# Second attention in blocks of one key block, values in four strips of 32 columns, and limits chosen head by head

## The chip, the core and the metric

The kernel runs on one core of a Trainium2 chip. The metric is the device time of one execution in microseconds (us). The engines are TensorE (PE in rows; PEld are its weight loads), VectorE (DVE), ScalarE (ACT), GpSimd (POOL) and SyncE, which only issues DMAs here. They run on their own and meet at semaphores.

## The reference, cut to what matters

The program is a model of two layers over 2 sequences of 1024 tokens with 1024 features: a token map, attention, a mixture of experts, and the same two again. The change is in the attention of the second layer, which keeps only the 128 highest scores of each row:

```python
draft = jnp.einsum('bhqd,bhkd->bhqk', qr, kr)
draft = draft + jnp.where(causal_future, neg, 0.0)
_, draft_indices = jax.lax.top_k(draft, 128)
mask = jnp.full((B, H, Sq, Sq), neg, dtype)
mask = mask.at[b_idx, h_idx, s_idx, draft_indices].set(0.0)
mask = jnp.where(causal_future[None, None, :, :], neg, mask)
scores = jnp.einsum('bhqd,bhkd->bhqk', qr, kr) / np.sqrt(HD) + mask
out = jnp.einsum('bhqk,bhkd->bhqd', jax.nn.softmax(scores, axis=-1), v)
```

There are 32 heads of 32 features in each sequence, four to a group of keys and values.

## The kernel before

`kept_attention` (from L825) works on pairs of heads, 32 pairs in all. For each head a row tile i (128 queries, i from 0 to 7) has i + 1 key blocks of 128 columns. The pairs pass through a pipeline of four stages, and one **slot** of the program does all four for four different pairs, so that 30 slots of 32 have every stage: *score* the pair s + 1, *search* the limits of pair s, *keep* (rank, choose and mark) pair s - 1, and *value* pair s - 2.

A slot is cut into five **passes**, 0 to 4. In each, ScalarE counts for 12 row tiles how many scores lie above a trial limit (`count`, L1076), VectorE then corrects the limits (`narrow`, L1253 to L1283, 11 short instructions in passes 1 to 3), and ScalarE's next count waits for that (`t_ready`). After pass 4 there is no correction: VectorE works out the first limits of the next pair instead (`start`, L1228 to L1249), from statistics of its scores (`gather`, L1226). ScalarE and VectorE thus take turns five times a slot, and whatever VectorE still has to do when a count ends makes the next count late.

Into the counts of passes 0, 1 and 2 ScalarE puts the evacuations of the value stage (`evac`, L1044): the exponential of a *chunk*, from one of two PSUM banks (`ps_t`) to SBUF (`probT`). There are 24 chunks in a slot, eight to a pass, of which five stand among the counts and three behind the last of them. A chunk before is up to four key blocks of one row tile of one head, and the chunks stand in pairs of the two heads. Their widths in blocks of 128 are 1, 1, 2, 2, 3, 3, 4, 4 in pass 0, 4, 4, 1, 1, 4, 4, 2, 2 in pass 1 and 4, 4, 3, 3, 4, 4, 4, 4 in pass 2.

TensorE fills a chunk (`turn`, L976): it transposes the score blocks, adds the negative maximum of each row (`row_of` times `topT`, L984) and adds the mask, transposed too (L989). A turn waits until the chunk two before it is evacuated. Behind each pair of turns stand the values of the pair before (`values`, L1001): [V | ones], 64 columns of weights for each head, times a 128-column block of `probT`, in float32; the two heads use the two halves of the array's columns. The profile has each float32 matmul as two rows. Among the turns of pass 2 TensorE also scores the first row tiles of the pair s + 1, two at a time ahead of the turns 16, 18 and 20, and the rest after its last values. The scores have two large banks (`ps_s`), and TensorE waits until VectorE has copied the tile two before (`fetch`, L1346, and `x_ready`).

VectorE's other work in a slot: it ranks (`rank_some`, L1297 on; L1291 and L1294 for each row tile) 8 of 14 tiles in pass 0 and 6 in pass 1, fetches scores 0 to 5, learns whether any row failed (`any_failing`) and marks 10 tiles (`mark`, L1338) in pass 2, marks 4, fetches 6 to 11 and copies the output in pass 3, and fetches 12 to 15 in pass 4. Fetches of passes 3 and 4 have statistics (`gather`) between them. GpSimd chooses the limits of all 14 tiles at once (`choose`, L1100), from the end of the ranking on, and later splits the row maxima in three parts (`split_top`, L1151). These are turned by TensorE and brought to SBUF by ScalarE at the end of pass 3 (`top_evac`, L1046), for the turns of the next slot.

A line number of GpSimd or VectorE names the instruction, and L1257 is the first of a correction, L1283 its last, L1244 the one that releases the first count of a slot.

## Time and profile before

| | us |
|---|---|
| median of 3 runs (lowest to highest) | 5007.57 (5001.28 to 5016.76) |
| the profiled execution | 5014.9 |
| its span | 5013.0 |
| PE busy in the span | 4052.5 (81%) |
| DVE busy | 3267.8 (65%) |
| ACT busy | 2800.5 (56%) |
| POOL busy | 311.6 (6%) |

The span begins with the first instruction of the profile and ends with the last. The page has a line for each engine with the busy tenths of 40 slices: in those of the second attention ACT and DVE stand at 7 and 8 tenths, PE at 6 and 7, and the clock granted to TensorE at 7 and 8 tenths. A timeline row has start, duration, engine, line, what is written and read, and how many instructions it merges; in brackets stands how long the engine was idle before, and who released it.

### The profile page before, as it was taken

The page shows a single profiled execution, that of the slowest core. Times are in us where ns is not written, and L with a number is a line of the kernel's source. Part 1 is how long each engine was busy: PE and PEld are TensorE (multiplying, and loading weights), DVE is VectorE, ACT ScalarE, POOL GpSimd, SP SyncE. Part 2 cuts the span into 40 slices and gives each one's busy share as a digit, 9 for nine tenths or more (in the row PEclk, how much of TensorE's full clock was granted, in tenths as well). Part 3 has the DMA queues.
Part 4 walks back from the last instruction along what each step waited for, and adds up shares of the span by engine and source line. Part 5 has one row for each costly group of instructions (what it writes and reads, how often), then busy time and mean ns, then how long its engine had stood idle before and what let it go on. Part 6 is the DMA issues. An engine that isn't in the chain of part 4 may idle for free. (4 is left out here: it accounts for less than half of the span.)

```text
span 5013.0 us, 84271 instructions
## 1 busy us (share of the span) xinstructions
PE 4052.5 (81%) x25752; PEld 2330.3 (46%) x25752; DVE 3267.8 (65%) x9570; ACT 2800.5 (56%) x6546; POOL 311.6 (6%) x1173
## 2 busy tenths in 40 slices
PE   6998999999999999945777466766766776676899
PEld 2445766667444444412444234433443443444454
DVE  2555777777233345558877787787788778886344
ACT  1114777777000011158888488888888888887100
POOL 1000000000000000001101001101110110111000
PEclk9999999999999999966777678778887877886899
DMA  3326323232211112320111011111011111000542
GB/s 142 78 66 167 81 55 76 60 76 54 93 50 50 54 44 66 85 47 11 28 28 24 4 28 28 24 28 27 6 28 28 28 24 28 12 20 6 127 116 78
DMA packets 308427, 260.27 MB, mean 52 GB/s; under 512 B 188672, under 2 KB 242704, under 8 KB 307920
## 3 DMA queue, kind: packets, MB, share of 16 engines
q1 hardware_dynamic: 307376, 254.32, 20.0%
q8 instruction: 210, 3.44, 0.3%
q14 instruction: 297, 2.43, 0.2%
q0 software_dynamic: 544, 0.07, 0.0%
HBM read 176.21 MB, written 78.12 MB: 51 GB/s over the span
## 5 line engine op out<-in xcount | busy, mean ns | idle before, releaser
L1076 ACT ACTIVATE a_sign<-arena,a_state 128x384 fp8e4<-128x384 f32 (+5 forms) x1056 | 917.9, 870 | 120.3 <-DVE a_state L1283 59.3
L970 PE MATMUL a_ps_s<-k,q 128*128 128x512 bf16 (+3 forms) x1536 | 414.9, 408 | 400.0 <-DVE arena L1346 263.2
L982 PE MATMUL a_ps_t<-ident,arena 128*128 128x128 f32 x1584 | 346.3, 337 | 281.2 <-ACT a_probT L1044 264.7
L1044 ACT ACTIVATE a_probT<-a_ps_t 128x512 f32<-128x512 f32 (+3 forms) x768 | 360.0, 477 | 221.0 <-PE a_ps_t L989 215.3
L1076 ACT ACTIVATE a_sign<-a_third,a_state 128x384 fp8e4<-128x384 f32 (+2 forms) x480 | 417.2, 871 | 87.7 <-DVE a_state L1283 75.2
L738 ACT ACTIVATE a_prob<-a_x_neg,a_shift 128x640 f32<-128x640 f32 (+7 forms) x512 | 397.2, 776 | 87.1 <-DVE a_x_neg L781 63.1
L970 PEld LDWEIGHTS a_ps_s<-k,q 128*128 128x128 bf16 x1536 | 146.8, 116 | 580.2 <-DVE arena L1346 297.2
L781 DVE TENSOR_SCALAR_CACHE_REDUCE a_x_neg<-a_ps_s 128x640 f32<-128x640 f32 (+7 forms) x512 | 378.8, 752 | 40.3 <-PE a_ps_s L662 25.8
L677 PE MATMUL a_ps_t<-ident,a_prob 128*128 128x128 f32 x2304 | 364.7, 282 | 36.4 <-issue 13.4
L1294 DVE MAX8 a_nine<-a_below 128x8 f32<-128x256 f32 (+6 forms) x448 | 371.2, 828 | 34.4 <-issue 1.7
L1008 PE MATMUL a_ps_o<-a_probT,vals 128*64 128x128 f32 x4608 | 385.7, 312 | 0.0
L982 PEld LDWEIGHTS a_ps_t<-ident,arena 128*128 128x128 f32 x1584 | 207.0, 168 | 362.4 <-ACT a_probT L1044 311.1
L1346 DVE TENSOR_SCALAR_CACHE_REDUCE arena<-a_ps_s 128x128 f32<-128x128 f32 (+7 forms) x352 | 259.7, 753 | 161.8 <-PE a_ps_s L973 158.3
L659 PE MATMUL a_ps_s<-k,q 128*128 128x512 bf16 (+3 forms) x1536 | 338.1, 330 | 19.2 <-DVE a_bias_b L773 11.8
L350 PE MATMUL p_ps_qkv<-arena,p_hT 128*128 128x512 f32 x768 | 337.3, 596 | 1.2 <-ACT p_hT L384 1.2
L350 PE MATMUL p_ps_qkv<-wqkv,p_hT 128*128 128x512 f32 x768 | 336.3, 595 | 1.2 <-ACT p_hT L384 1.2
L791 DVE COPY a_probT<-a_ps_t 128x384 f32<-128x384 f32 (+3 forms) x384 | 221.7, 577 | 169.3 <-PE a_ps_t L677 167.7
L1008 PEld LDWEIGHTS a_ps_o<-a_probT,vals 128*64 128x64 f32 x4608 | 284.0, 154 | 45.1 <-issue 20.5
L677 PEld LDWEIGHTS a_ps_t<-ident,a_prob 128*128 128x128 f32 x2304 | 249.5, 142 | 105.9 <-issue 39.6
L984 PE MATMUL a_ps_t<-a_topT,a_row_of 48*128 48x512 bf16 (+3 forms) x768 | 297.3, 387 | 0.0
L989 PE MATMUL a_ps_t<-a_ident_b,a_mask 128*128 128x128 bf16 x2240 | 283.4, 247 | 0.0
L982 PE MATMUL a_ps_t<-ident,a_third 128*128 128x128 f32 x720 | 160.8, 343 | 128.4 <-ACT a_probT L1044 114.9
(263 smaller groups left out, 6778.9 us busy)
## 6 DMA issues: line engine op xcount, KB each, us to landing
q<-qk SPq DMA_DIRECT2D x256, 256.0 KB, 4.6
qk<-p_qkT SPq DMA_DIRECT2D x32, 960.0 KB, 6.2
h_rows<-h SPq DMA_DIRECT2D x32, 512.0 KB, 6.9
k<-qk SPq DMA_DIRECT2D x256, 64.0 KB, 4.8
h<-tok_h SPq DMA_DIRECT2D x16, 512.0 KB, 4.0
arena<-in_wo SPq DMA_DIRECT2D x16, 512.0 KB, 6.5
o<-a_o SPq DMA_DIRECT2D x16, 512.0 KB, 2.7
q<-o SPq DMA_DIRECT2D x16, 512.0 KB, 5.6
```

The costliest lines, as they stand in the source:

```text
L350: m = nc.tensor.matmul(ps_qkv[:, n * BANK:(n + 1) * BANK], hT[:, par, k * P:(k + 1) * P], w[:, k, n * BANK:(n + 1) * BANK], start=(k == 0) ...
L659: nc.tensor.matmul(ps_s[:, s % 2, a:a + w], q[:, x, y, m, i * P:(i + 1) * P], k[:, x, y, a:a + w], start=(y == 0), stop=False, skip_group_ ...
L677: mm = nc.tensor.transpose(ps_t[:, n % 2, c * P:(c + 1) * P], prob[:, s % 2, (a + c) * P:(a + c + 1) * P], ident[:, :])
L738: nc.scalar.activation(prob[:, s % 2, 0:w], x_neg[:, s % 4, 0:w], ACT.Exp, scale=-1.0, bias=shift[:, s % 4:s % 4 + 1], accum_out=total[:, ...
L781: nc.vector.tensor_scalar(x_neg[:, c, 0:w], ps_s[:, s % 2, 0:w], -1.0, None, ALU.mult, ALU.min, accum_out=shift[:, c:c + 1]).then_inc(shif ...
L970: nc.tensor.matmul(ps_s[:, n % 2, a:a + w], q[:, y, head, i * P:(i + 1) * P], k[:, y, a:a + w], start=(y == 0), stop=False, skip_group_che ...
L982: nc.tensor.matmul(to[:, c:c + P], xs[old][:, at:at + P], ident[:, :], start=(c == 0), stop=False, is_transpose=True, skip_group_check=True)
L984: mm = nc.tensor.matmul(to.rearrange("p (b c) -> p b c", c=P), row_of[:, m * TT + i, :], topT[:, :].unsqueeze(1).to_broadcast([SPLITS * 2 ...
L1008: mm = nc.tensor.matmul(ps_o[half:half + 2 * DH, i * P:(i + 1) * P], v[:, at, :], probT[:, (n + m) % 4, b * P:(b + 1) * P], start=(at == 0 ...
L1044: nc.scalar.activation(probT[:, n % 4, 0:w], ps_t[:, (n + 1) % 2, 0:w], ACT.Exp).then_inc(probT_ready, 1)
L1076: ins = nc.scalar.activation(to, xs[mine][:, at:at + w], ACT.Sign, scale=-1.0, saturate=False, bias=state[:, par, 0, n:n + 1], accum_out=s ...
L1294: lambda: nc.vector.max(nine[:, n, 1:9], below[:, r, 0:w]),
```

## The change

- The chunks hold **one key block b** of up to four row tiles (i0 on) of one head, in place of one row tile's key blocks. There are still 24, with the same widths in another order: the table below has them.
- `values` is 4 matmuls for a pair of chunks, each of 32 columns of weights (V or ones, of either head) and up to 512 columns of data, in place of 64 columns of weights and 128 of data: 48 matmuls a slot in place of 72.
- The row maxima get one matmul a chunk as before, from `topT_wide` (48 x 8 x 128), which GpSimd makes of `topT` in a new step `widen`, after `top_evac`. The turns of a slot wait for it (`widened`).
- `choose` runs once for each head, with 7 tiles, the first after the 7 tiles of the first head are ranked (pass 0; 7 more in pass 1). What tells VectorE of failing rows is a step behind both (`tell_failing`, `told`).
- The first 8 scores use four small banks. They are scored in two groups of four, ahead of the turns 16 and 20.
- VectorE marks 12 tiles in pass 2 (three of each head first, when that head's limits are there, then after the flag and two fetches six more, each when the turns have read the old mask) and 2 in pass 3. Six statistics stand in pass 3 in place of four.

| pass | widths before | widths now |
|---|---|---|
| 0 | 1 1 2 2 3, 3 4 4 | 4 4 4 4 3, 3 4 4 |
| 1 | 4 4 1 1 4, 4 2 2 | 2 2 4 4 1, 1 4 4 |
| 2 | 4 4 3 3 4, 4 4 4 | 4 4 3 3 2, 2 1 1 |

The comma parts the five evacuations among the counts from the three behind them.

```diff
+    SPANS = [(b, max(b, i0), i0 + HALF_T - max(b, i0)) for b in range(TT) for i0 in (0, HALF_T) if b < i0 + HALF_T]
+    CH = [(n, m, b, i0, c * P) for n, (m, b, i0, c) in enumerate(
+        (m, b, i0, c) for b, i0, c in SPANS for m in range(2))]
...
+        EARLY = {16: range(0, 4), 20: range(4, NARROW)}
+        turned = {b: 2 + n for n, m, b, i0, w in CH if b == i0}
...
+            if n < NARROW:
+                return ps_s[:, n % 4 // 2, n % 2 * BANK:(n % 2 + 1) * BANK]
...
-                        mm = nc.tensor.matmul(to.rearrange("p (b c) -> p b c", c=P), row_of[:, m * TT + i, :],
-                                              topT[:, :].unsqueeze(1).to_broadcast([SPLITS * 2 * TT, w // P, P]),
+                        mm = nc.tensor.matmul(to, head_of[:, m, :],
+                                              topT_wide[:, :, :].rearrange("p i c -> p (i c)")[:, i0 * P:i0 * P + w],
...
-                        for b in range(w // P):
+                        for d in (0, DH):
                             for m in range(2):
-                                half, at = 2 * m * DH, a // P + b
-                                mm = nc.tensor.matmul(ps_o[half:half + 2 * DH, i * P:(i + 1) * P], v[:, at, :],
-                                                      probT[:, (n + m) % 4, b * P:(b + 1) * P], start=(at == 0),
-                                                      stop=(at == i), tile_position=(0, half))
+                                half = 2 * m * DH + d
+                                mm = nc.tensor.matmul(ps_o[half:half + DH, i0 * P:i0 * P + w], v[:, b, d:d + DH],
+                                                      probT[:, (n + m) % 4, 0:w], start=(b == 0), stop=(b == i0),
...
+                        pe.wait_ge(widened, s - 1)
...
+                    def widen():
+                        wait_alone(pool, probT_ready, (s - 1) * TURNED + 1, const_in, 48)
+                        nc.gpsimd.tensor_tensor(topT_wide[:, :, :], topT[:, :].unsqueeze(1).to_broadcast([SPLITS * 2 * TT, TT, P]),
+                                                own[:, :].unsqueeze(2).to_broadcast([SPLITS * 2 * TT, TT, P]),
+                                                ALU.mult).then_inc(widened, 1)
...
-                        choose()
+                        choose(0)
+                        choose(1)
+                        tell_failing()
+                        widen()
...
+                                for r in KEEPS[0]:
+                                    if r in SHORT:
+                                        dve.wait_ge(chosen, s * 2 + (RANKED[r][0] - 1))
+                                    mark(r).then_inc(mask_ready, 1)
+                                dve.wait_ge(told, s)
+                                any_failing()
...
+                                for r in KEEPS[1][0:SOON]:
+                                    if st["value"]:
+                                        dve.wait_ge(turn_done, (s - 2) * TURNED + turned[RANKED[r][1]])
+                                    mark(r).then_inc(mask_ready, 1)
```

TensorE at the start of a value stage, before: turns of one block and of two, then values in pairs of 64 columns.

```order
L982 MATMUL a_ps_t<-ident,arena 128x128 [waits a1_probT_ready,a1_mask_ready,v_in]
L984 MATMUL a_ps_t<-a_topT,a_row_of 128x128
L982 MATMUL a_ps_t<-ident,arena 128x128 [waits a1_probT_ready]
L984 MATMUL a_ps_t<-a_topT,a_row_of 128x128
L982 MATMUL a_ps_t<-ident,arena 128x128 [waits a1_probT_ready]
L982 MATMUL a_ps_t<-ident,arena 128x128
L984 MATMUL a_ps_t<-a_topT,a_row_of 128x256
L989 MATMUL a_ps_t<-a_ident_b,a_mask 128x128 x2
L982 MATMUL a_ps_t<-ident,arena 128x128 [waits a1_probT_ready]
L982 MATMUL a_ps_t<-ident,arena 128x128
L984 MATMUL a_ps_t<-a_topT,a_row_of 128x256
L989 MATMUL a_ps_t<-a_ident_b,a_mask 128x128 x2
```

And now: the first four turns have four blocks each.

```order
L995 MATMUL a_ps_t<-ident,arena 128x128 [waits a1_probT_ready]
L995 MATMUL a_ps_t<-ident,arena 128x128 x3
L997 MATMUL a_ps_t<-a_topT_wide,a_head_of 128x512
L1003 MATMUL a_ps_t<-a_ident_b,a_mask 128x128 x4
L995 MATMUL a_ps_t<-ident,arena 128x128 [waits a1_probT_ready]
L995 MATMUL a_ps_t<-ident,arena 128x128 x3
L997 MATMUL a_ps_t<-a_topT_wide,a_head_of 128x512
L1003 MATMUL a_ps_t<-a_ident_b,a_mask 128x128 x4
L1022 MATMUL a_ps_o<-a_probT,vals 32x512 [waits a1_probT_ready]
L1022 MATMUL a_ps_o<-a_probT,vals 32x512 x3
```

The order of turns and values is the same, and the wide ones come first.

VectorE in pass 2, before (`a_mask` are the marks, `a_ps_s` the scores):

```order
L1346 TENSOR_SCALAR a_third,a_top<-a_ps_s 128x128 [waits a1_s_done,a1_top_ready]
L1346 TENSOR_SCALAR a_third,a_top<-a_ps_s 128x128 [waits a1_s_done]
L1346 TENSOR_SCALAR a_third,a_top<-a_ps_s 128x256 [waits a1_s_done] x2
L1346 TENSOR_SCALAR a_third,a_top<-a_ps_s 128x384 [waits a1_s_done] x2
L1307 STREAM_TRANSPOSE a_codeT<-a_code 128x32 [waits a1_chosen]
L1310 CAST a_codes<-a_codeT 1x32 x4
L1312 TENSOR_REDUCE a_failing<-a_codes 1x1
L1338 TENSOR_SCALAR a_mask<-arena,a_limit 128x256 x2
L1338 TENSOR_SCALAR a_mask<-arena,a_limit 128x384 x2
L1338 TENSOR_SCALAR a_mask<-arena,a_limit 128x512 x2
L1338 TENSOR_SCALAR a_mask<-arena,a_limit 128x640 x2
L1338 TENSOR_SCALAR a_mask<-arena,a_limit 128x768 x2
```

And now, from the third fetch on (two fetches of 128 columns stand ahead, two marks of 896 behind):

```order
L1378 TENSOR_SCALAR arena,a_top<-a_ps_s 128x256 [waits a1_s_done] x2
L1370 TENSOR_SCALAR a_mask<-a_third,a_limit 128x256 [waits a1_chosen]
L1370 TENSOR_SCALAR a_mask<-a_third,a_limit 128x384
L1370 TENSOR_SCALAR a_mask<-a_third,a_limit 128x512
L1370 TENSOR_SCALAR a_mask<-a_third,a_limit 128x256 [waits a1_chosen]
L1370 TENSOR_SCALAR a_mask<-a_third,a_limit 128x384
L1370 TENSOR_SCALAR a_mask<-a_third,a_limit 128x512
L1339 STREAM_TRANSPOSE a_codeT<-a_code 128x32 [waits a1_told]
L1342 CAST a_codes<-a_codeT 1x32 x4
L1344 TENSOR_REDUCE a_failing<-a_codes 1x1
L1378 TENSOR_SCALAR arena,a_top<-a_ps_s 128x384 [waits a1_s_done] x2
L1370 TENSOR_SCALAR a_mask<-a_third,a_limit 128x640 [waits a1_turn_done] x2
```

Six marks stand ahead of the flag, and each head's first mark waits for its own `chosen`.

GpSimd after the limits, before:

```order
L1145 TENSOR_TENSOR a_limit<-a_kept_on,a_all_on 128x14
L1147 TENSOR_TENSOR a_marked<-a_marked 128x4
L1147 TENSOR_TENSOR a_marked<-a_marked 128x2
L1149 TENSOR_TENSOR a_code<-a_marked 128x1
L1155 TENSOR_SCALAR a_neg<-a_top 128x16 [waits a1_x_ready]
L1157 CAST a_top_b<-a_neg 128x16
L1159 CAST a_top_parts<-a_top_b 128x16
L1160 TENSOR_TENSOR a_rest<-a_neg,a_top_b 128x16
```

And now, between `tell_failing` and the splitting of the maxima:

```order
L1158 TENSOR_TENSOR a_limit<-a_kept_on,a_all_on 128x7
L1162 TENSOR_TENSOR a_marked<-a_fail,bits 128x14
L1165 TENSOR_TENSOR a_marked<-a_marked 128x8
L1165 TENSOR_TENSOR a_marked<-a_marked 128x4
L1165 TENSOR_TENSOR a_marked<-a_marked 128x2
L1167 TENSOR_TENSOR a_code<-a_marked 128x1
L1172 TENSOR_TENSOR a_topT_wide<-a_topT,a_own 48x1024 [waits a1_probT_ready]
L1180 TENSOR_SCALAR a_neg<-a_top 128x16 [waits a1_x_ready]
L1182 CAST a_top_b<-a_neg 128x16
```

One instruction of 48 x 1024 stands between the two steps of the program before.

## Rows read from the trace of the kernel before

**Rows 1.** One line: the output copy, one a slot, first and last start.

```profile
L1354 DVE COPY a_o<-a_ps_o x32: 1205/1207/1225, 2383.3 to 4687.9; 128x1024 f32<-128x1024 f32 x32
```

**Rows 2.** Timeline (start, duration in us) of ScalarE and VectorE, pass 0.

```profile
3056.21 0.25 ACT L1044 ACTIVATE a_probT<-a_ps_t 128x128 f32<-128x128 f32 x1
...
3065.80 0.19 ACT L1076 ACTIVATION_READ_ACCUMULATOR a_sign<-a_third,a_state 128x1 f32 x1
...
3066.76 0.41 DVE L1291 SCALAR_TENSOR_TENSOR a_below<-a_last,arena 128x256 f32<-128x256 fp8e4 x1
...
3067.87 0.17 DVE L1257 TENSOR_TENSOR a_state<-a_state,search 128x14 f32<-128x14 f32 x1 [0.20 <-issue]
...
3069.50 0.60 ACT L1044 ACTIVATE a_probT<-a_ps_t 128x512 f32<-128x512 f32 x1 [1.34 <-PE a_ps_t L989]
```

**Rows 3.** Timeline of TensorE: turns and values at either clock.

```profile
3003.55 1.97 PE L1008 MATMUL a_ps_o<-a_probT,vals 128*64 128x128 f32 x16
...
3018.43 1.09 PE L1008 MATMUL a_ps_o<-a_probT,vals 128*64 128x128 f32 x16
...
3065.34 1.12 PE L982 MATMUL a_ps_t<-ident,arena 128*128 128x128 f32 x4
...
3067.32 1.06 PE L982 MATMUL a_ps_t<-ident,arena 128*128 128x128 f32 x4
...
3069.39 1.55 PE L1008 MATMUL a_ps_o<-a_probT,vals 128*64 128x128 f32 x12
```

**Rows 4.** Timeline of TensorE in the first attention.

```profile
803.67 2.17 PE L691 MATMUL a_ps_o<-a_probT,vals 128*32 128x128 f32 x72
```

**Rows 5.** Busy time of engines by stretch, then the granted clock.

```profile
3066.00:3071.90 5.90, 5.90 (x33) 3.52 (x31) 4.68 (x20) 3.35 (x8) 0.00 (x0) 0.50 0.00 1
3071.90:3082.00 10.10, 8.08 (x76) 5.11 (x76) 9.07 (x15) 9.56 (x24) 0.47 (x3) 1.00 0.01 2
```

**Rows 6.** Timeline of pass 2: GpSimd, VectorE, and the end of the count.

```profile
3009.29 0.19 POOL L1106 TENSOR_SCALAR a_state<-a_over 128x2 f32<-128x2 f32 x1 [32.81 <-DVEq L1303]
...
3018.09 0.21 POOL L1145 TENSOR_TENSOR a_limit<-a_kept_on,a_all_on 128x14 f32<-128x14 f32 x1
...
3020.05 0.56 DVE L1346 TENSOR_SCALAR_CACHE_REDUCE a_third<-a_ps_s 128x384 f32<-128x384 f32 x1 [3.24 <-PE a_ps_s L973]
...
3022.44 4.05 DVE L1338 TENSOR_SCALAR a_mask<-arena,a_limit 128x256 bf16<-128x256 f32 x10
...
3024.91 0.19 ACT L1076 ACTIVATION_READ_ACCUMULATOR a_sign<-arena,a_state 128x1 f32 x1
...
3026.76 0.17 DVE L1257 TENSOR_TENSOR a_state<-a_state,search 128x14 f32<-128x14 f32 x1 [0.27 <-issue]
```

**Rows 7.** Timeline of passes 3 and 4, the same engines.

```profile
3029.80 2.60 DVE L1338 TENSOR_SCALAR a_mask<-arena,a_limit 128x896 bf16<-128x896 f32 x4
...
3039.52 0.24 ACT L1048 CAST a_topT<-a_ps_t 48x128 bf16<-48x128 f32 x1
...
3040.23 0.17 DVE L1257 TENSOR_TENSOR a_state<-a_state,search 128x14 f32<-128x14 f32 x1 [0.17 <-issue]
...
3042.22 0.18 DVE L1283 COPY_PREDICATED a_state<-a_open,a_new 128x14 f32<-128x14 int32 x1
...
3048.86 2.68 DVE L1226 BATCH_NORM_STATS2 a_stats<-a_third 128x6 f32<-128x160 f32 x6
```

**Rows 8.** Timeline where a GpSimd and a VectorE instruction meet.

```profile
3083.10 0.38 POOL L1117 TENSOR_TENSOR a_hot<-iota,a_rank 128x112 f32<-128x112 f32 x1
3083.13 0.40 DVE L1258 TENSOR_TENSOR a_side<-a_state 128x28 int32<-128x28 f32 x1
```

**Rows 9.** Timeline of choosing and narrowing side by side, pass 1 to pass 2.

```profile
3009.97 0.22 POOL L1112 TENSOR_TENSOR a_state<-a_state,search 128x14 f32<-128x14 f32 x1 [0.16 <-issue]
3010.01 0.20 DVE L1257 TENSOR_TENSOR a_state<-a_state,search 128x14 f32<-128x14 f32 x1 [0.91 <-ACT a_sign L1076]
...
3011.95 0.18 DVE L1283 COPY_PREDICATED a_state<-a_open,a_new 128x14 f32<-128x14 int32 x1
```

185 lines of the change are left out of this document (102 added, 83 removed).

## The prediction

> **What bounds the kernel now.** The page first: over the second attention neither ScalarE nor VectorE nor TensorE is full, so no share of busy time is the bound. The rows of the output copy give the slot: 32 copies, the first at 2383.3 us, the last at 4687.9, which is (4687.9 - 2383.3) / 31 = 74.3 us a slot [rows 1]. Then the timeline of one slot, engine by engine, and in it what ends last before each count. It is a ring of ScalarE (count) and VectorE (correction), and the reader should look for three kinds of lateness in it.
>
> In pass 0 the count ends at 3065.80 + 0.19 = 3065.99, and VectorE begins its correction only at 3067.87, 1.9 late, since it still ranks its eighth tile from 3066.76 on. But ScalarE does not gain by an earlier correction alone: its last evacuation, 3069.50 to 3070.10, waited 1.34 for TensorE's turn [rows 2]. In pass 2 the count ends at 3024.91 + 0.19 = 3025.10, and the correction begins at 3026.76, 1.66 late. VectorE stood 3.24 waiting for its last two scores, and only then read the flag and made ten marks, 4.05 [rows 6]. In pass 3 the count is over as the copy of the maxima begins, 3039.52, plus the 0.1 by which the two overlap, and the correction begins at 3040.23, 0.6 late [rows 7]. TensorE is at 1.2 GHz (granted 0.50) in the stretch 3066.0 to 3071.9 and at 2.4 GHz (1.00) in the next [rows 5].
>
> **The values.** Four strips of 32 columns are in the trace already: the first attention does 9 blocks of 128 columns for four heads in 72 rows and 2.17 us, 0.24 a block; the second does 4 blocks for two heads in 16 rows and 1.09 at the high clock, 0.27 a block [rows 3, 4]. So strips run side by side, and time goes with the columns of data, which stay the same. Fewer, longer matmuls: 0, at most 0.03 x 18 pairs of blocks of TensorE off the path.
>
> **Pass 0.** The five evacuations among the counts grow from 9 blocks to 19. A block costs (0.60 - 0.25) / 3 = 0.12 [rows 2], so the count ends 1.2 later, at 3067.2. VectorE loses the eighth ranking (at most 3067.87 - 3066.76 = 1.1) and is ready then: the correction begins 0.7 earlier than now. What is late next is TensorE. At the low clock a turn of four blocks is 3067.32 - 3065.34 = 1.98, values of four blocks 1.97, of three 1.55 [rows 3], a turn of three about 1.5. From the first evacuation (56.2 to 56.8, in us after 3000): turn 2 to 58.8, evacuation 1 to 59.3, turn 3 to 61.3, values to 63.3, turns 4 and 5 to 66.3, values to 68.3, turns 6 and 7 to 72.3, last evacuation to 73.0, against 70.1 now: **+2.9** if the clock stays low. But these values stand at 61.3, and now the first long values of this part stand at 69.39, just before the clock rose at 71.9; the other low stretch likewise held values of 1.97 at 3003.55, and at 3018.43 they take 1.09 [rows 3, 5]. If it rises at about 65, turn 5, values, turns 6 and 7 take half: 65 + 0.9 + 1.1 + 1.0 + 1.0 + 0.7 = 69.7: **-0.4**. I take **0**, nearer to the early rise, because the engine is denser than now from 3057 on; +2.9 and -0.4 stay as bounds. The 0.7 is swallowed.
>
> **Pass 1.** Same evacuation work (14 blocks to 13). VectorE ranks a tile more (1.1) where it waited 0.91 for the count [rows 9]. The last two chunks have 4 blocks in place of 2, but their turns have the whole correction to hide in. **0**, bounds -0.2 to +0.6.
>
> **Pass 2.** The four scores stand ready in four banks, so the wait of 3.24 goes. Next late is GpSimd: limits took from 3009.29 to 3018.30 [rows 6]; with 7 tiles and without two instructions of the flag about 1 less, 3017.2. Three marks, 1.1, to 3018.4; the flag is five small steps behind the limits, 3018.9; reading it took 1.35 (from 3020.05 + 2 x 0.5 for two fetches to 3022.44), to 3020.3; two fetches 1.0; six marks at about 0.55 (4.05 / 10 and 2.60 / 4, rows 6 and 7, bracket it) 3.3, to 3024.6; the last check 0.27: 3024.9 [rows 6, 7]. The count ends 0.2 earlier than now (18 blocks to 16), 3024.9. The whole 1.66 + 0.2 would go; VectorE's longer pass 1 may start the limits up to 0.9 late. I take **-1.4**, bounds -1.9 and -0.5.
>
> **Pass 3.** Two marks leave (2.60 / 4 x 2 = 1.3), two statistics come (2.68 / 6 x 2 = 0.9), and the lateness of 0.6 shrinks to about 0.1: **-0.5**, bounds -0.6 and -0.3 [rows 7].
>
> **`widen`.** It can start when the maxima are copied, 3039.76, so at about 3039.9, in the midst of the correction that now begins at 3039.65. A GpSimd instruction on two inputs takes 0.22 for 14 columns and 0.38 for 112 [rows 8, 9], 0.0016 a column: 1024 columns make 0.22 + 1010 x 0.0016 = 1.9 us. TensorE does not need it before the last scores of pass 4 are done, whose statistics begin at 3048.86 [rows 7]; VectorE may be held by it. In rows 8 its instruction of 0.17 began 0.03 behind GpSimd's, took 0.40, and ended at 3083.53, right after GpSimd's end at 3083.48. Held so, the correction stops at its third or fourth instruction until 3041.8 and ends at 3043.6 in place of 3041.8: **+1.8**. The other end is rows 9: a whole correction beside small GpSimd instructions took 3012.13 - 3010.01 = 2.12, while one alone in pass 3 took 42.40 - 40.23 = 2.17, so no cost. I take +1.8, since a single long instruction can't be slipped past as small ones can; bounds 0 and +2.5 (if its end or its columns are dearer).
>
> The Trainium skill, SBUF — State Buffer, section "Who interferes with whom", says that a VectorE instruction with two SBUF inputs and a GpSimd instruction that reads SBUF exclude each other, each for its whole length. By that rule, with which rows 8 agree and rows 9 hardly show, `widen` costs the +1.8; with rows 9 alone the change would gain 69 us.
>
> **Pass 4.** One of the two statistics that left stood behind the last fetch, where VectorE's chain ends: 2.68 / 6 = 0.45, taken **-0.4**, bounds -0.5 and 0 [rows 7].
>
> **The sum.** 0 + 0 - 1.4 - 0.5 + 1.8 - 0.4 = -0.5 a slot; 30 slots have every stage: -15 us. The profiled execution took 5014.9 (span 5013.0 and 1.9 around it): 4999.9. The median of the runs is 7.3 below it: **4993**. The slots at either end, with stages missing, I take as unchanged.
>
> **Rivals.** (a) *`widen` holds nobody*: -2.3 a slot, -69, **4938**. For it: rows 9. Against: rows 8. Chance 0.18. (b) *TensorE stays at the low clock through pass 0*, and count 1 waits for the last evacuation. Decides from the point where turn 7 ends later than about 3069.5 on the scale above. Each slot where it holds pays +2.9. In half of them: +1.45 - 0.5 = +0.95, +29, **5036**; in all: +72, 5080. For it: the clock stayed low to 3071.9 with TensorE busy 5.90 of 5.90. Against: the earlier, longer values. Chance 0.22, the main way to a slower kernel. (c) *The limits come late and pass 2 keeps its lateness*: VectorE's seventh ranking in pass 1 delays `ranked`, GpSimd's second choice, marks and flag; +1.4 - 0.5 = +0.9, +27, **5034**. Chance 0.12. (d) *The four strips do not run side by side at 512 columns*: values(0) and values(2) of pass 0 double, +3.9 on the chain of pass 0, +100, about **5110**. Against: rows 4. 0.04. (e) *The clock is high in most of passes 1 and 2*, since TensorE is denser at the start: up to -0.8 a slot more, **4970**, 0.06. The forecast itself keeps 0.38, its own range 4978 to 5008.
>
> **How the numbers follow.** A measurement of this kernel can tell about 0.3% (15 us) from no change, so "same" is 4992.6 to 5022.6, and the forecast lies on its edge: of its 0.38 half counts as faster, half as same. Faster: 0.19 + 0.18 + 0.06, 0.43. Slower: 0.22 + 0.12 + 0.04 less a part in which (b) holds in few slots only, 0.33. Same: 0.24. The range goes from (a) to a little over (b) in half of the slots, 4935 to 5045.
>
> **What would show it.** Right: a GpSimd row of 48 x 1024 of about 1.9 us just behind the copy of the maxima; a VectorE instruction of the correction of pass 3 stretched to its end; the correction of pass 2 beginning within 0.4 of the count's end; that of pass 0 too, with the first count of pass 1 still waiting for an evacuation. Wrong: an undisturbed correction in pass 3 (a), the low clock with four or more us between the correction and the next count in pass 1 (b), marks waiting for GpSimd in pass 2 (c), values of a four-block pair over 2 us at the high clock (d).

## The result, and the profile after

| | before | after |
|---|---|---|
| median of 6 runs each (us) | 5009.16 | 5028.07 |
| lowest to highest | 4990.28 to 5016.76 | 5026.04 to 5028.77 |
| span of the profiled execution | 5013.0 | 5025.6 |

The ratio is 1.0042, with a 95% interval of 1.0025 to 1.0060: about 0.4% slower (19 us between the medians), against the 4993 that were predicted. (Before has 3 more runs here than in the table ahead of the prediction.)

The copies of the output, which answer to [rows 1], give (4701.4 - 2379.4) / 31 = 74.9 us a slot in place of 74.3.

```profile
L1386 DVE COPY a_o<-a_ps_o x32: 1198/1207/1224, 2379.4 to 4701.4; 128x1024 f32<-128x1024 f32 x32
```

The question is in which pass that is. (In the fences of rows below, rows that stand between those shown are left out.) The table below is worked out from the trace's instructions, as a mean over 28 slots with every stage (the one of about 130 us, in which a row is selected exactly, is left out for both). Where a cell has two numbers, they are before and after. "Count" goes from the first to the last instruction of ScalarE's count, "late" (the lateness) from there to the first instruction of VectorE's correction, "wait" from the correction's end to the next count's first instruction. The wait is 0.08 where nothing else is in the way. Behind count 4 there is no correction, and "late" is all that VectorE still does then.

| pass | count | late | correction | wait | sum before | sum after | difference | predicted |
|---|---|---|---|---|---|---|---|---|
| 0 | 11.91, 12.98 | 2.23, 0.36 | 1.31, 1.32 | 0.50, 0.96 | 15.95 | 15.62 | -0.33 | 0 |
| 1 | 12.79, 12.33 | 0.03, 0.06 | 2.38, 2.23 | 0.08, 1.54 | 15.28 | 16.16 | +0.88 | 0 |
| 2 | 13.93, 13.62 | 1.64, 1.31 | 2.15, 2.15 | 0.08, 0.08 | 17.80 | 17.16 | -0.64 | -1.4 |
| 3 | 10.67, 10.67 | 0.58, 0.03 | 2.21, 3.75 | 0.08, 0.08 | 13.54 | 14.53 | +0.99 | +1.3 |
| 4 | 10.67, 10.67 | 0.89, 0.66 | | 0.08, 0.08 | 11.64 | 11.41 | -0.23 | -0.4 |

The sum is +0.67 in place of -0.5. Two terms are wrong by about 0.8 each: pass 1 and pass 2.

**Pass 1.** The last of the count in ScalarE, in a slot that starts at 3126.1 (columns as in [rows 2]):

```profile
3153.73 0.19 ACT L1091 ACTIVATION_READ_ACCUMULATOR a_sign<-arena,a_state 128x1 f32 x1
3153.82 0.26 ACT L1059 ACTIVATE a_probT<-a_ps_t 128x128 f32<-128x128 f32 x1
3155.67 0.60 ACT L1059 ACTIVATE a_probT<-a_ps_t 128x512 f32<-128x512 f32 x1 [1.59 <-PE a_ps_t L1003]
3157.60 0.60 ACT L1059 ACTIVATE a_probT<-a_ps_t 128x512 f32<-128x512 f32 x1 [1.33 <-PE a_ps_t L1003]
3158.10 0.61 ACT L1091 ACTIVATE a_sign<-arena,a_state 128x384 fp8e4<-128x384 f32 x1
```

TensorE in the same place, and the clock granted to it in three stretches (the columns of the window rows are the stretch, its length, the busy time of PE, PEld, DVE, ACT and POOL with their instructions, the granted clock, and the DMA):

```profile
3150.74 0.47 PE L995 MATMUL a_ps_t<-ident,arena 128*128 128x128 f32 x1 [1.95 <-ACT a_probT L1059]
3151.58 1.93 PE L1022 MATMUL a_ps_o<-a_probT,vals 128*32 128x512 f32 x8
3142.00:3147.00 5.00, 4.19 (x32) 1.96 (x30) 4.71 (x13) 5.00 (x13) 3.90 (x9) 1.00 0.00 0
3150.00:3153.00 3.00, 2.26 (x11) 0.59 (x11) 2.93 (x4) 3.00 (x9) 0.07 (x1) 0.51 0.00 0
3153.00:3160.00 7.00, 7.00 (x44) 4.21 (x41) 3.90 (x22) 4.08 (x10) 4.70 (x18) 0.50 0.01 2
```

The count ends at 3153.92, and the first count of pass 2 begins at 3158.10, since the two evacuations of four blocks wait 1.59 and 1.33 for their turns. These turns stand behind values of four blocks (1.93), and at the low clock (1.2 GHz), which begins at 3150.1, in the middle of an idle stretch of TensorE of 1.95 (3148.79 to 3150.74).

One of the 28 slots has the high clock from 4337.9 to 4372.1, so through all of this. The same place in it:

```profile
4352.48 0.33 PE L995 MATMUL a_ps_t<-ident,a_third 128*128 128x128 f32 x1 [1.95 <-ACT a_probT L1059]
4355.56 0.96 ACT L1059 ACTIVATE a_probT<-a_ps_t 128x128 f32<-128x128 f32 x2
4357.22 0.60 ACT L1059 ACTIVATE a_probT<-a_ps_t 128x512 f32<-128x512 f32 x1 [0.70 <-PE a_ps_t L1003]
4357.85 0.61 ACT L1091 ACTIVATE a_sign<-arena,a_state 128x384 fp8e4<-128x384 f32 x1
4352.00:4360.00 8.00, 7.06 (x63) 4.04 (x63) 6.53 (x26) 7.17 (x18) 3.66 (x14) 1.00 0.01 3
```

The correction ends at 4357.82 and the count begins at 4357.85: with the same order of chunks and the high clock, nothing waits. So the wait of pass 1 is the price of the low clock there. The idle stretch of 1.95 stands in this slot too, and the clock did not fall, so that stretch alone does not bring the fall.

**Pass 2.** VectorE, from its first fetch to the correction, which answer to [rows 6]:

```profile
3158.62 0.29 DVE L1378 TENSOR_SCALAR_CACHE_REDUCE arena<-a_ps_s 128x128 f32<-128x128 f32 x1 [1.47 <-PE a_ps_s L986]
3160.36 2.28 DVE L1370 TENSOR_SCALAR a_mask<-a_third,a_limit 128x256 bf16<-128x256 f32 x6
3163.07 0.21 DVE L1339 STREAM_TRANSPOSE a_codeT<-a_code 128x32 f32<-128x32 f32 x1 [0.43 <-POOL a_code L1167]
3164.15 0.27 DVE L1344 TENSOR_REDUCE a_failing<-a_codes 1x1 int32<-1x128 int32 x1
3167.00 0.56 DVE L1378 TENSOR_SCALAR_CACHE_REDUCE arena<-a_ps_s 128x384 f32<-128x384 f32 x1 [2.58 <-PE a_ps_s L986]
3167.96 3.26 DVE L1370 TENSOR_SCALAR a_mask<-a_third,a_limit 128x640 bf16<-128x640 f32 x6
3173.12 0.17 DVE L1289 TENSOR_TENSOR a_state<-a_state,search 128x14 f32<-128x14 f32 x1 [1.89 <-issue]
3171.69 0.19 ACT L1091 ACTIVATION_READ_ACCUMULATOR a_sign<-arena,a_state 128x1 f32 x1
```

The count ends at 3171.88. The six marks end before that, at 3171.22, and yet the correction begins at 3173.12, 1.89 later, with nothing that the row could name as a releaser ("issue"). Ahead of it stand a wait of 0.43 for GpSimd's flag and one of 2.58 for score 4.

**Pass 3.** GpSimd's `widen`, and the correction beside it, which answers to [rows 7]:

```profile
3186.25 1.89 POOL L1172 TENSOR_TENSOR a_topT_wide<-a_topT,a_own 48x1024 bf16<-48x1024 bf16 x1 [23.21 <-ACT a_topT L1063]
3185.99 0.17 DVE L1289 TENSOR_TENSOR a_state<-a_state,search 128x14 f32<-128x14 f32 x1 [0.43 <-ACT a_sign L1091]
3186.43 1.79 DVE L1294 COPY_PREDICATED a_bracket<-a_side,a_state 128x56 f32<-128x56 int32 x1
3189.55 0.18 DVE L1315 COPY_PREDICATED a_state<-a_open,a_new 128x14 f32<-128x14 int32 x1
```

`widen` takes 1.89 (estimate: 1.9), and the fourth instruction of the correction takes 1.79 and ends 0.08 behind it.

### The profile page after: what moved, and what is told of

It is laid out like the page before. It is cut to its first block and busy times, and to the rows that moved or that the text cites. A ratio compares the mean times of both kernels' runs of the same rounds, so it can differ in the third digit from the quotient of the medians.

```text
span 5025.6 us, 82526 instructions
## 1 busy us (share of the span) xinstructions
PE 4004.6 (80%) x24075; PEld 2133.6 (42%) x24216; DVE 3314.9 (66%) x9572; ACT 2799.6 (56%) x6546; POOL 632.7 (13%) x1909
## 5 line engine op out<-in xcount | busy, mean ns | idle before, releaser
L995 PE MATMUL a_ps_t<-ident,arena 128*128 128x128 f32 x1584 | 334.8, 330 | 248.3 <-ACT a_probT L1059 225.2
L983 PEld LDWEIGHTS a_ps_s<-k,q 128*128 128x128 bf16 x1536 | 170.1, 128 | 683.8 <-DVE arena L1378 335.4
L677 PE MATMUL a_ps_t<-ident,a_prob 128*128 128x128 f32 x2304 | 364.7, 282 | 35.5 <-issue 15.6
L1022 PE MATMUL a_ps_o<-a_probT,vals 128*32 128x512 f32 (+3 forms) x3072 | 374.2, 571 | 0.0
L997 PE MATMUL a_ps_t<-a_topT_wide,a_head_of 48*128 48x512 bf16 (+3 forms) x768 | 289.2, 377 | 0.0
L1091 ACT ACTIVATE a_last<-arena,a_state 128x384 fp8e4<-128x384 f32 (+5 forms) x264 | 229.1, 869 | 81.3 <-DVE a_state L1315 79.8
L384 ACT COPY p_hT<-p_ps_h 128x512 f32<-128x512 f32 x64 | 34.4, 589 | 408.5 <-PE p_ps_h L337 408.5
```

The costliest lines, as they stand in the source:

```text
L677: mm = nc.tensor.transpose(ps_t[:, n % 2, c * P:(c + 1) * P], prob[:, s % 2, (a + c) * P:(a + c + 1) * P], ident[:, :])
L983: nc.tensor.matmul(score(n)[:, a:a + w], q[:, y, head, i * P:(i + 1) * P], k[:, y, a:a + w], start=(y == 0), stop=False, skip_group_check= ...
L995: nc.tensor.matmul(to[:, c * P:(c + 1) * P], xs[old][:, at:at + P], ident[:, :], start=(c == 0), stop=False, is_transpose=True, skip_group ...
L997: mm = nc.tensor.matmul(to, head_of[:, m, :], topT_wide[:, :, :].rearrange("p i c -> p (i c)")[:, i0 * P:i0 * P + w], start=False, stop=Fa ...
L1022: mm = nc.tensor.matmul(ps_o[half:half + DH, i0 * P:i0 * P + w], v[:, b, d:d + DH], probT[:, (n + m) % 4, 0:w], start=(b == 0), stop=(b == ...
L1091: ins = nc.scalar.activation(to, xs[mine][:, at:at + w], ACT.Sign, scale=-1.0, saturate=False, bias=state[:, par, 0, n:n + 1], accum_out=s ...
```

## Experiments

All ratios are to the kernel before, with their 95% intervals, and the time in us is the median. For the changed kernel as it is they are 1.0042 and 5028. The waits and latenesses are means over the same slots as above. The kernel before was run again beside each group of runs, with medians from 5004.8 to 5013.4, so a time may differ by some 9 us from one group to another, and the ratios are the better comparison.

### What the wait before the correction of pass 2 is

The records of VectorE's sequencer, which the busy rows leave out, have a register load and a branch in that gap: `exact_where_needed` loads the flag into a register and, where no row failed, branches over the exact selection of 14 row tiles. In the slots shown, in us:

```
before: branch 3023.12, next instruction 3025.92; ten marks run from 3022.44 to 3026.49
after:  register load 3169.68, branch 3170.03, next instruction 3172.84; marks run until 3171.22
```

The branch takes 2.8 in both. Before, the marks cover it. The theory was that in the changed kernel the sequencer reaches it too late, because the last two marks wait for turn 21. First its price by itself, in the kernel before, with the branch moved ahead of the ten marks:

```diff
                                 with dve.If_ne(this, 0):
                                     select_exactly(n)
-                                    if n in KEEPS[2]:
-                                        mark(n)
...
                                 any_failing()
+                                exact_where_needed()
                             for r in keeps:
                                 mark(r).then_inc(mask_ready, 1)
-                            if keeps:
-                                exact_where_needed()
```

> The kernel before with one step moved: VectorE branches over the exact selection right behind the flag, ahead of the ten marks in place of behind them. Theory: the taken branch takes 2.7 us of the sequencer and was free only because ten marks (4.1 us) were queued ahead of it. Now nothing is queued, and each of 30 slots is 2.5 to 2.7 longer: 5009 + 78 = 5087. Rival: the branch is cheap, or overlaps whatever stands around it: 5009 within 10.

Measured: 5125.8, 1.0242 (1.0217 to 1.0267), even more than the 5087 that were expected. The lateness of pass 2 went from 1.64 to 5.01 and that of pass 3 from 0.58 to 1.06. VectorE behind the flag, and ScalarE's end of the count:

```profile
3202.17 0.27 DVE L1312 TENSOR_REDUCE a_failing<-a_codes 1x1 int32<-1x128 int32 x1
3205.90 4.05 DVE L1338 TENSOR_SCALAR a_mask<-a_third,a_limit 128x256 bf16<-128x256 f32 x10 [3.46 <-issue]
3210.17 0.17 DVE L1257 TENSOR_TENSOR a_state<-a_state,search 128x14 f32<-128x14 f32 x1 [0.22 <-issue]
3205.00 0.19 ACT L1076 ACTIVATION_READ_ACCUMULATOR a_sign<-arena,a_state 128x1 f32 x1
```

Load and branch uncovered cost 3.46, where the expectation had 2.5 to 2.7. The opposite is to leave them out of the changed kernel, with all that the branch skips:

```diff
                     def exact_where_needed():
 
-                        dve.reg_load(which, failing[:, :])
-                        with dve.If_ne(which, 0):
...
                         dve.nop()
                         dve.drain()
```

> The changed kernel without the exact selection: the register load, the branch and all that it skips are left out, so rows whose limit failed are not selected exactly (this leaves out a part of the computation, which runs in one of the 30 slots and takes 54 us there). Theory: each of the other slots has the branch's 1.2 us of lateness in pass 2, so the time is 5028 - 54 - 29 x 1.2 = 4939. Rival: scores 4 and 5, turn 21 and the marks behind them set the end of pass 2 and the branch is not on the path: 5028 - 54 = 4974.

Measured: 4939.6, 0.9872 (0.9855 to 0.9889), against 4939 by the theory. Some 54 us of the gain are the exact selection itself, which this kernel leaves out. The lateness of pass 2 is 0.04 in the mean of 29 slots; the marks now end before the count does, and the correction waits for ScalarE:

```profile
3098.34 3.26 DVE L1370 TENSOR_SCALAR a_mask<-a_third,a_limit 128x640 bf16<-128x640 f32 x6
3102.28 0.17 DVE L1289 TENSOR_TENSOR a_state<-a_state,search 128x14 f32<-128x14 f32 x1 [0.68 <-ACT a_sign L1091]
```

So all of the 1.3 is the load and the branch. That is shown; how to cover it again was harder. The first move, right behind the flag and ahead of the wait for score 4:

```diff
-                                    if n in KEEPS[0] or n in KEEPS[1][0:SOON]:
+                                    if n in KEEPS[0]:
...
                                 any_failing()
+                                exact_where_needed()
                             if st["score"]:
                                 for n in MORE:
...
-                                exact_where_needed()
                             dve.drain()
```

> The changed kernel with one step moved: VectorE branches over the exact selection right behind the flag, ahead of its fetches of scores 4 and 5 and of the last six marks, and no longer behind them. Theory: the lateness of 1.3 us that is left in pass 2 is the taken branch (2.7 us in the records), which nothing hides now, since the last marks wait for turns and the sequencer reaches the branch with them. Moved, it lies under the wait for score 4 (2.6 us), the correction of pass 2 begins within 0.2 of the count's end, and 1.1 to 1.3 a slot goes: 5028 - 30 x 1.2 = 4992. Rival: scores 4 and 5 and the turns that the marks wait for set the end of VectorE's work, and the branch only shows there; then nothing changes, 5028 within 6. A second rival: the branch costs as much where it stands now as where it stood, 2.7 ahead of the fetch, and the marks end later by what the wait does not cover: 5028 to 5045.

Measured: 5024.4, 1.0038 (1.0025 to 1.0051): nothing gained. The time is as the first rival had it; the rows show the mechanism of the second.

```profile
3162.82 0.27 DVE L1344 TENSOR_REDUCE a_failing<-a_codes 1x1 int32<-1x128 int32 x1
3164.59 0.22 PE L986 MATMUL a_ps_s<-a_bias_b,a_ident_b 128*128 128x128 bf16 x1
3166.65 0.56 DVE L1378 TENSOR_SCALAR_CACHE_REDUCE arena<-a_ps_s 128x384 f32<-128x384 f32 x1 [3.55 <-PE a_ps_s L986]
```

Score 4 ends at 3164.8, and its fetch begins at 3166.65: in this slot the wait that was to cover the branch is 1.7, not the 2.6 of the row above, and load and branch take 3.55. Next, the branch behind four of the six marks:

```diff
-                                    if n in KEEPS[0] or n in KEEPS[1][0:SOON]:
+                                    if n in KEEPS[0] or n in KEEPS[1][0:AHEAD]:
...
                                 for r in KEEPS[1][0:SOON]:
+                                    if r == KEEPS[1][AHEAD]:
+                                        exact_where_needed()
...
-                                exact_where_needed()
```

`AHEAD` is 4.

> The changed kernel with the branch over the exact selection moved ahead of the last two of the six marks behind the flag (it stood behind all six). Moved right behind the flag it was no better, because there it was waited for in full: the flag ended at 3163.1 and the next fetch began at 3166.65, 3.55 idle, after score 4 had long been done. Theory: here two fetches and four marks (3 us) are queued when the sequencer reaches the branch, since it no longer has to wait for turn 21 first, and two marks follow it; the 2.7 us are hidden, the correction of pass 2 begins 0.1 behind the count's end in place of 1.3, and each slot loses 1.2: 5028 - 36 = 4992. Rival: the correction of pass 2 is late because of scores 4 and 5 and turns 20 and 21 themselves; then nothing changes, 5028 within 6, as after the first move.

Measured: 5046.5, 1.0078 (1.0061 to 1.0095), slower than where it stood; both the theory and the rival were wrong. In most slots the lateness fell to about 0.7, but in every sixth (always the last body of the loop, the same place in the code) it was 3.0 to 3.2:

```profile
2944.16 2.07 DVE L1370 TENSOR_SCALAR a_mask<-a_third,a_limit 128x640 bf16<-128x640 f32 x4
2949.80 1.28 DVE L1370 TENSOR_SCALAR a_mask<-a_third,a_limit 128x896 bf16<-128x896 f32 x2 [3.57 <-PE a_ps_t L1003]
2945.54 0.28 PE L1003 MATMUL a_ps_t<-a_ident_b,a_mask 128*128 128x128 bf16 x2
```

Turn 21 was done at 2945.8, and the records have the instruction behind the branch at 2947.08 and the next one only at 2949.70: a second stall of 2.6 behind the first. Even so the mean lateness is 1.07 in place of 1.31, and pass 2 as a whole is as long as in the changed kernel (17.1 against 17.2). The 0.7 by which the slot is longer stands elsewhere, most of it in the waits behind passes 0 and 1 (1.19 and 1.76 in place of 0.96 and 1.54). Then five short branches in place of the long one:

```diff
-                            for n in range(NS):
-                                dve.reg_alu(this, which, 1 << n, ALU.bitwise_and)
...
+                        for at in range(0, NS, 4):
+                            with dve.If_ne(which, 0):
+                                for n in range(at, min(at + 4, NS)):
+                                    dve.reg_alu(this, which, 1 << n, ALU.bitwise_and)
...
```

> The changed kernel, with the one branch over the exact selection of all 14 tiles replaced by a branch over its first step and four over at most four tiles each; the place and the work are the same. In the one slot where a row fails, a branch over one tile's selection takes 0.2 us in the records, where the one over all 14 takes 2.7. Theory: what is dear is the length of the jump (code that has not been fetched ahead), and five short ones take about 1 us in all: lateness of pass 2 from 1.3 to 0.3, 5028 - 30 = 4998. Rival: a jump over four tiles is as dear as one over 14, and five of them follow each other: each slot up to 4 x 2.7 longer, 5028 + 300. Second rival: they are short and nothing is gained, as the branch is not on the path: 5028.

> As with branches over four tiles each, but over two tiles each, so eight branches. Theory: at 0.2 to 0.25 each they take 1.6 to 2 us: lateness of pass 2 about 0.8, 5028 - 15 = 5013. If jumps over four tiles are dear and over two are not, this one alone is faster. Rival, that the branch is not on the path: 5028.

Measured: 5040.3, 1.0073 (1.0054 to 1.0091) and 5074.6, 1.0135 (1.0117 to 1.0154), lateness 1.83 and 2.76. Both expectations were wrong, and the records of four tiles each say why:

```
branches at 3172.81, 3173.03, 3173.55, 3173.74, 3176.16; correction at 3176.58
```

The first three jumps took 0.2 to 0.5, and the fourth 2.4. So it is not the length of one jump that is dear, but the code that is skipped in all. The reading is that after some of it the sequencer runs out of what was fetched ahead and waits once; no record shows the fetching itself. Cutting the branch only adds to that.

The last question was what makes the sequencer late. Scores 6 and 7 stand ahead of turn 20, so they were moved behind turn 21:

```diff
-        EARLY = {16: range(0, 4), 20: range(4, NARROW)}
+        EARLY = {16: range(0, 4), 20: (4, 5), 22: (6, 7)}
```

> The changed kernel, where TensorE scores 6 and 7 ahead of turn 22 in place of turn 20; scores 4 and 5 stay ahead of turn 20. Theory: the branch is uncovered because the last two marks wait for turn 21, and turn 21 stands behind scores 6 and 7 (1.25 us): in the trace it ends 2.3 after score 5, of the 3 us that two fetches and four marks last. With scores 6 and 7 behind it, it ends 1.2 earlier, the sequencer reaches the branch 1.2 earlier, and the lateness of pass 2 goes from 1.3 to 0.1 though the branch stands where it stood: 5028 - 36 = 4992. Rival: what counts is the number of marks behind the branch's last wait, two as before, or the order of the marks; nothing changes: 5028 within 6.

Measured: 5035.5, 1.0043 (1.0026 to 1.0060), where 4992 was expected. The theory of the scores fell: lateness 1.16. Turn 21 no longer waits for them, but for the evacuation in ScalarE's count behind which it stands, and it ends at 3172.5 all the same (the register load is at 3172.56, the count's end at 3174.93):

```profile
3171.64 0.44 PE L995 MATMUL a_ps_t<-ident,arena 128*128 128x128 f32 x2 [0.58 <-ACT a_probT L1059]
3175.98 0.17 DVE L1289 TENSOR_TENSOR a_state<-a_state,search 128x14 f32<-128x14 f32 x1 [1.69 <-issue]
```

All early scores in pairs, as before:

```diff
+        EARLY = {16: (0, 1), 18: (2, 3), 20: (4, 5), 22: (6, 7)}
```

> The changed kernel with the early scores two at a time as before: 0 and 1 ahead of turn 16, 2 and 3 ahead of 18, 4 and 5 ahead of 20, 6 and 7 ahead of 22. Theory: beside the gain of moving scores 6 and 7 (36 us), turn 16 stands behind two scores in place of four (0.7 to 1.1 us less), so the evacuation of chunk 16 waits less and the count of pass 2 ends up to 0.5 earlier; scores 2 and 3 are still there before the first marks could start: 5028 - 36 - 10 = 4982, between 4975 and 4992. Rival: scores 2 and 3 behind turn 17 hold VectorE's first marks and so the flag, and everything behind it is later: 5000 to 5028.

Measured: 5027.4, 1.0029 (1.0018 to 1.0041). The count of pass 2 is 0.4 shorter (13.21), as expected, the lateness 1.12, as with scores 6 and 7 moved, and count 2 begins 0.2 later than in the changed kernel. Pass 2 is 0.6 shorter in all, and passes 0, 1 and 4 are 0.2 longer each. No gain by the time. At last the wait itself was taken away, with the two marks of row tile 6 in pass 3:

```diff
-        HALF, SOON, NARROW = 4, 6, TT
+        HALF, SOON, NARROW = 4, 4, TT
```

> The changed kernel with four marks behind the flag in pass 2 and four in pass 3, in place of six and two: the two marks of row tile 6, which wait for turn 21, go to pass 3, and the branch stays the last step of pass 2. With scores 6 and 7 moved behind turn 21, that turn waited for evacuation 19 in ScalarE's count instead, the register load of the branch still began 0.06 behind turn 21, and the lateness stayed at 1.16: so the branch's place in time is the wait on turn 21 itself. Theory: without that wait the sequencer reaches the branch with score 5, the lateness of pass 2 goes from 1.3 to 0.05, and of the 1.3 us of marks that pass 3 gets, 0.4 to 0.9 shows there as lateness (it has 0.4 of slack and two waits of 0.3): -0.4 to -0.8 a slot, 5010, between 5004 and 5016. Rival: the branch is late whatever stands ahead of it; then pass 2 keeps 1.2 and the time is 5028 + 10 to 25.

Measured: 5024.1, 1.0030 (1.0018 to 1.0041), where 5004 to 5016 was expected. The mechanism is as expected: the register load is at 3167.71, ahead of the first of the four marks (3167.98), and the lateness of pass 2 is 0.06, with the branch in its old place. But pass 3 has 0.96 of lateness in place of 0.03. Passes 2 and 3 together are 0.4 shorter, passes 0 and 1 are 0.2 longer each, and the slot is no shorter. **The branch is exposed by the wait on turn 21**: in this order of the chunks row tile 6 is read until turn 21, and a branch behind its marks starts too late to be covered. The other way, with those marks in pass 3, gives most of it back there.

### What `widen` costs

```diff
                         wait_alone(pool, probT_ready, (s - 1) * TURNED + 1, const_in, 48)
+                        if st["search"]:
+                            wait_alone(pool, t_ready, s * PASSES + PASSES, const_in, 48)
```

> The changed kernel, where widen also waits until the correction of pass 3 has released the count of pass 4; nothing else differs. Theory: GpSimd's 48 x 1024 instruction of 1.9 us holds VectorE's instructions on two inputs, so the correction of pass 3 takes 3.75 in place of 2.2. Behind the correction it meets fetches and statistics, which have one input, and costs nothing: -1.5 a slot, 5028 - 46 = 4982. Rival: the correction of pass 3 is long for another reason (the copy of the maxima, or what stands ahead on VectorE), and moving widen changes nothing: 5028 within 6. Between: it holds VectorE in pass 4 too, where VectorE ends last, and half or more of the gain comes back: 4995 to 5028.

Measured: 5023.5, 1.0033 (1.0022 to 1.0043). The correction of pass 3 is back at 2.19, and the end of pass 4 went from 0.66 to 2.43: the third of the outcomes, and all of the gain came back.

```profile
3183.82 1.89 POOL L1174 TENSOR_TENSOR a_topT_wide<-a_topT,a_own 48x1024 bf16<-48x1024 bf16 x1 [25.28 <-DVE a_state L1317]
3183.82 2.30 DVE L1252 TENSOR_SCALAR a_last<-arena,a_state 128x256 fp8e4<-128x256 f32 x2
```

The two short counts take 2.30; beside nothing they take 0.62. They read one tensor in SBUF and have no accumulator. The Trainium skill has this: SBUF — State Buffer, section "Who interferes with whom", lists `tensor_scalar` without an accumulator among the instructions that can take the pair of ports shared with GpSimd, where their operands allow it, and so be blocked. The trace agrees: the two are held for 1.68, of the 1.89 that `widen` takes. Without `widen`, each block's maxima again get a matmul of their own:

```diff
-                        mm = nc.tensor.matmul(to, head_of[:, m, :],
-                                              topT_wide[:, :, :].rearrange("p i c -> p (i c)")[:, i0 * P:i0 * P + w],
-                                              start=False, stop=False, skip_group_check=True)
+                        for c in range(w // P):
+                            mm = nc.tensor.matmul(to[:, c * P:(c + 1) * P], row_of[:, m * TT + i0 + c, :], topT[:, :],
+                                                  start=False, stop=False, skip_group_check=True)
...
-                        widen()
```

> The changed kernel without widen and topT_wide: each block of a chunk gets its own matmul of 128 columns with row_of and topT, as in the kernel before (up to four in place of one of 512 columns; the output is the same). Theory: widen costs VectorE 1.55 a slot wherever it stands near the count (in the correction of pass 3 it held one instruction for 1.79; put behind the correction it held the short counts of pass 4, 2.30 in place of 0.62), and four matmuls of 128 columns take as long as one of 512, as the mask's do. So the correction of pass 3 is back at 2.2 and nothing is lost elsewhere: 5028 - 46 = 4982. Rival: the 24 more weight loads and matmuls a slot make each wide turn 0.1 to 0.3 longer, at the low clock above all, and the evacuations behind passes 0 and 1 wait for them: +0.5 to +1 a slot, 5000 to 5015. Second rival: what the correction of pass 3 gives back is lost in pass 4, as when widen was moved: 5028.

Measured: 4972.3, 0.9927 (0.9906 to 0.9948), where 4982 was expected. Correction 3 takes 2.19, pass 4 ends at 0.84, and the matmuls of the maxima are as cheap as the theory had it (289.5 us in all for 2304 of 128 columns, against 289.2 for 768 of 128 to 512; that is 48 more a slot, not the 24 of the expectation). Without this one term the change is 0.7% faster in place of 0.4% slower.

### The end of pass 1

```diff
+    SPANS[6], SPANS[7] = SPANS[7], SPANS[6]
```

> The changed kernel with two pairs of chunks exchanged: widths in pass 1 are 2 2 4 4 4, 4 1 1 in place of 2 2 4 4 1, 1 4 4. Theory: the first count of pass 2 begins 1.5 late because the two chunks behind the last count of pass 1 are four blocks wide and are turned at the low clock behind values of four blocks; with one block each it begins on time, but VectorE's chain in pass 2 (scores, limits, turns) is not much earlier, so most of it comes back as lateness of the correction: -0.4 a slot, 5016, between 5028 and 4998. Rival: the whole chain of pass 2 moves with the count, -1.4 a slot, 4986. A second rival: the wide turns now make the evacuations among the counts of pass 1 late, and nothing is gained: 5028 or more.

Measured: 4988.7, 0.9968 (0.9956 to 0.9980). The rival was right: count 2 begins on time (wait 0.09), the lateness of pass 2 stays at 1.34, and the whole pass moves.

```profile
3144.24 0.74 ACT L1060 ACTIVATE a_probT<-a_ps_t 128x512 f32<-128x512 f32 x2
3145.55 0.28 ACT L1060 ACTIVATE a_probT<-a_ps_t 128x128 f32<-128x128 f32 x1 [0.58 <-PE a_ps_t L1004]
3146.59 0.61 ACT L1092 ACTIVATE a_sign<-arena,a_state 128x384 fp8e4<-128x384 f32 x1 [0.76 <-DVE a_state L1316]
3138.00:3146.00 8.00, 5.62 (x48) 2.44 (x40) 6.40 (x16) 7.18 (x17) 3.44 (x14) 1.00 0.01 2
```

The clock of this stretch is 1.00, where it was 0.50. Over the 28 slots, the mean granted clock from 24 to 34 us into the slot is 0.59 in the changed kernel and 0.88 here. Sorted by that clock, passes 1 and 2 together take as long in either order:

| granted clock, 24 to 34 us into the slot | changed kernel | chunks exchanged |
|---|---|---|
| under 0.53 | 33.9 (18 slots) | 34.1 (1 slot) |
| between | 32.5 (9) | 32.5 (15) |
| over 0.99 | 30.5 (1) | 31.4 (12) |

So, as far as these slots show, the exchange gains by keeping the clock high in more of them, and not by the width of the last chunks. In the one slot with the low clock, count 2 does begin with a wait of 0.34 only, but an evacuation inside it waits 2.62 for its turn, and the pass is longer by that. Two cells have one slot each. Why this order keeps the clock high is not shown.

### Values in four strips or in two halves

```diff
-                        for d in (0, DH):
-                            for m in range(2):
-                                half = 2 * m * DH + d
+                        for m in range(2):
+                            half = 2 * m * DH
...
```

> The changed kernel, where the values of a pair of chunks are 2 matmuls with 64 columns of weights (values and ones of one head) in place of 4 with 32; still up to 512 columns of data. Theory: matmuls in different column strips run side by side, and time goes with the columns of data, so the values of a four-block pair stay at 1.07 (high clock) and nothing changes: 5028 within 8. Rival: four short strips are what makes the new values quick, and two halves take longer; then a four-block pair takes up to 2.1, and passes 0 and 1 grow: 5060 or more. Opposite rival: weight loads and starts of four matmuls cost something: up to 10 us less.

Measured: 5038.2, 1.0070 (1.0053 to 1.0087). Four blocks take the same in two halves:

```profile
3133.43 1.93 PE L1022 MATMUL a_ps_o<-a_probT,vals 128*32 128x512 f32 x8
3137.67 1.06 PE L1022 MATMUL a_ps_o<-a_probT,vals 128*32 128x512 f32 x8
3132.36 1.97 PE L1021 MATMUL a_ps_o<-a_probT,vals 128*64 128x512 f32 x4
3136.59 1.08 PE L1021 MATMUL a_ps_o<-a_probT,vals 128*64 128x512 f32 x4
```

The median is 10 us above the changed kernel's, with intervals that overlap; the mean of all values of 512 columns is 0.758 in place of 0.732 for one row, and count 1 begins 0.3 later. So four strips cost nothing over two halves, and may gain a little.

### Repairs together

Each has the exchanged chunks and no `widen`, with the branch ahead of the last two marks (the first), in parts of four tiles, with scores 6 and 7 later, with all early scores in pairs, and that with two marks in pass 3:

> The changed kernel with three repairs at once: the two pairs of chunks of pass 1 exchanged (widths 2 2 4 4 4, 4 1 1; alone 39 us), the branch ahead of the last two marks, and no widen. Theory: the three stand in different passes and add up: 5028 - 39 - 36 - 46 = 4907. Rival: with the repairs the next thing is late (the last evacuations of pass 0, VectorE's end of pass 4, scores 0 to 3), and a third of it comes back: 4940. If the branch is not what makes pass 2 late: 4943.

> The changed kernel with the pairs of chunks exchanged, no widen, and branches over four tiles each in the place of the change. Theory: -39 and -55 as measured alone, -30 for the branches: 4904; where they meet, what is late next takes back a part, as before (the three repairs with the branch moved gave 4942 in place of 4907): 4904 to 4935. If jumps over four tiles are dear: 5100 or more.

> The changed kernel with scores 6 and 7 ahead of turn 22, the pairs of chunks of pass 1 exchanged and no widen; the branch stands where the change has it. Theory: 5028 - 39 - 55 - 36 = 4898 if they add up; the three repairs with the branch moved gave 4942, with 0.9 of lateness left in pass 2, of which 0.8 goes here: 4918. Rival: the lateness stays, 4942 or more.

> The changed kernel with the early scores two at a time, the pairs of chunks of pass 1 exchanged and no widen. Theory: as with scores 6 and 7 moved alone, and up to 10 less, since turn 16 is no longer behind four scores: 4908 to 4918. Rival: scores 2 and 3 come too late for VectorE, 4925 to 4945.

> The version with scores two at a time, the pairs of chunks of pass 1 exchanged and no widen (4929), with the two marks of row tile 6 in pass 3 too. Theory: pass 2 loses its 1.15 of lateness, pass 3 gets 0.4 to 0.9: 4929 - 7 to - 22, about 4915. Rival: as above, 4929 or more.

| | us | ratio (95%) | late in pass 2 | late in pass 3 |
|---|---|---|---|---|
| branch ahead of two marks | 4941.8 | 0.9870 (0.9854 to 0.9887) | 0.92 | 0.03 |
| branch in parts of four | 4957.0 | 0.9900 (0.9882 to 0.9919) | 2.07 | 0.03 |
| scores 6 and 7 later | 4937.4 | 0.9856 (0.9840 to 0.9872) | 1.13 | 0.03 |
| early scores in pairs | 4928.7 | 0.9835 (0.9819 to 0.9852) | 1.15 | 0.03 |
| that, two marks in pass 3 | 4931.0 | 0.9843 (0.9826 to 0.9859) | 0.04 | 0.92 |

All five came out above their expectations, of 4907, 4904 to 4935, 4918, 4908 to 4918 and 4915. The fourth beats both kernels, the one before by 1.65% and the changed one by about 99 us. Its copies of the output are (4600.7 - 2375.3) / 31 = 71.8 apart:

```profile
L1373 DVE COPY a_o<-a_ps_o x32: 1206/1207/1225, 2375.3 to 4600.7; 128x1024 f32<-128x1024 f32 x32
```

Alone, the exchange gave 39 and the kernel without `widen` 56, which add up to 95 of its 99 us; the two together, without the pairs of scores, were not run. The branch is not among them: its 1.15 a slot stays, and in the fifth it only changes place. How long each pass is, as means over the 28 slots:

| | pass 0 | 1 | 2 | 3 | 4 | slot |
|---|---|---|---|---|---|---|
| before | 15.9 | 15.3 | 17.8 | 13.5 | 11.6 | 74.2 |
| changed | 15.6 | 16.2 | 17.2 | 14.5 | 11.4 | 74.9 |
| branch ahead of two marks | 16.0 | 16.4 | 17.1 | 14.5 | 11.6 | 75.6 |
| early scores in pairs | 15.8 | 16.4 | 16.6 | 14.5 | 11.6 | 75.0 |
| two marks in pass 3 | 15.9 | 16.3 | 16.3 | 15.0 | 11.6 | 75.1 |
| no `widen` | 16.0 | 15.8 | 16.8 | 13.0 | 11.6 | 73.2 |
| chunks exchanged | 15.6 | 15.0 | 17.1 | 14.5 | 11.6 | 73.9 |
| fourth of the repairs | 16.0 | 15.1 | 16.1 | 13.0 | 11.6 | 71.7 |

Where the order of the chunks stayed, what pass 2 gained by moving the branch, the scores or the marks came back in good part as longer passes 0 and 1, where ScalarE waits for turns. So the lateness of one pass shows a mechanism, and only the slot shows its worth.

## Why the prediction was wrong, point by point

Two steps failed, by about 0.8 a slot each, pass 1 a little more than pass 2; together they turn the forecast gain into a loss.

- **Pass 2, -1.4, measured -0.64: a cost taken for covered.** The prediction's list ends with "the last check 0.27". That number is from rows in which ten marks cover the branch. Its size uncovered is 3.5, and here 1.3 of it is on the path. The rest of the list held in its end: the six marks end before the count does, and without the branch pass 2 has no lateness at all (0.04), as forecast. Its steps did not hold, and that the end came out is partly luck: in the slot shown the flag is read 7.45 before the count's end, where the sum had 4.6, and then VectorE waits 2.58 for score 4, which the list does not have. Rival (c) forecast the symptom (lateness kept), and its 5034 is the nearest number to 5028, but not the cause: the limits came early.
- **Pass 1, 0, measured +0.88, above its bound of +0.6: an overlap that holds at the high clock only.** "Their turns have the whole correction to hide in" is true in the one slot with the high clock (wait 0.04) and wrong in the others: turns 14 and 15 stand behind the values of a four-block pair, at the low clock, which takes 1.93 + 2 x 1.98 = 5.9 from 3151.6 on, and the last evacuation ends at 3158.2, where the correction ends at 3156.07. The rows for it were there: the price of four-block turns at the low clock is in [rows 3]. The prediction worked out both clocks in pass 0 and none in pass 1. A clock that is high through the end of pass 1, as in rival (e), came in one slot of 28.
- **Pass 0, 0, measured -0.33**, near the bound of -0.4 that stood for an early rise of the clock. The clock rose at 3136.4, 10.3 into the slot, where the sum had about 10.9; over the slots 8.6 to 10.7, against 12.3 to 19.2 in the kernel before. Rival (b) did not come.
- **`widen`, +1.8, measured +1.55**, by the mechanism of [rows 8]: one VectorE instruction held to its end. Rival (a) was wrong. The bound of 0, from small instructions, had no bearing on a long one. Undone, it is worth 56 us, more than 30 x 1.55 = 47: by the slots pass 3 gives 1.55 and passes 1 and 2 give 0.3 each, passes 0 and 4 take 0.55 back, and 30 slots of 1.67 are 50.
- **Pass 3 without it, -0.5, measured -0.55. Pass 4, -0.4, measured -0.23** (bounds -0.5 and 0).
- **Strips**: 1.06 and 1.93 for a four-block pair in place of 1.09 and 1.97, so rival (d) was wrong.
- The forecast lay on the edge of "same" with two unlike terms of 1.4 and 1.8 against each other. An error of 0.8 in one term was enough to turn its sign, and there were two of them, which the gains in passes 0 and 3 beyond the forecast made up for in part. The measured time lies within the wide range of 4935 to 5045, on the other side of no change.

## What to carry to other kernels

A price may be taken from a place where the step is covered only if the step will be covered in the new place too: ask of each branch and each register load what is queued ahead of it when the sequencer gets there. A wait in an instruction delays not only that instruction but also the sequencer's reading ahead, and so whatever comes behind with a latency of its own. And before a small helper on GpSimd is added beside a tight chain on VectorE, look whether TensorE can do it with constants at no cost.

## What the runs showed of the hardware

- A taken branch of VectorE over 14 tiles' selection takes 2.8, over one tile's (in the slot where a row fails) 0.2. Over 14 tiles in five parts it takes 0.2 to 0.5 three times and then 2.4. The jump back at the end of the loop's body costs as much: in the changed kernel the branch is at 2976.37 and the next instruction at 2979.17, and in the first slot behind each such jump the correction of pass 0 is 2.4 to 3.0 later than in the other slots, in both kernels. The Trainium skill, Runtime: NRT & Kernel Launch, section "Instruction fetch mechanics", says that instructions are fetched ahead in order, in pages, and that a taken branch out of what is held waits for its page. The traces agree, also in that the price is paid once and not by the number of branches; the price itself is from the traces.
- Behind such a branch a second stall of 2.6 can follow, in some places of the code and not in others (one slot of six).
- An instruction of 1.89 on GpSimd holds VectorE for 1.55 to 1.77 in both places where it was put, also short counts that read a single tensor.
- TensorE's granted clock at the end of pass 1 was 0.50 in the changed kernel and 1.00 with two pairs of chunks exchanged, in the slots shown, at the same work; as means over the slots 0.59 and 0.88, and over the whole span 0.872 and 0.883. In passes 1 and 2 the low clock cost 2.7 to 3.4 a slot against the high one (34.1 and 33.9 against 31.4 and 30.5).
